# Constant products on TensorE between the gated cell's last transposes and the shared experts' first gate product

## The chip, the core and the metric

The program runs on one core of one Trainium2 chip. The metric is the device time of one execution in microseconds (us). The core has a matrix engine (TensorE, PE in the profile, with its weight loads as PEld), VectorE (DVE), ScalarE (ACT), GpSimd (POOL) and a queue engine that issues transfers (SP). Each runs its own list of instructions in order; they meet through semaphores.

## What is computed

Two gated blocks on 16 sequences of 128 tokens with 256 channels, all in fp32. Cut to what matters here:

```python
x = x + tanh(g_xattn[0]) * L0_xattn(layernorm(x), ctx_1024, ...)   # gated mLSTM cell, 8 heads
x = x + tanh(g_ffn[0])   * L0_ffn(layernorm(x), ...)               # 2 shared + 8 routed experts, top 2
x = x + tanh(g_xattn[1]) * L1_xattn(layernorm(x), ctx_1024, ...)   # attention, 16 heads
x = x + tanh(g_ffn[1])   * L1_ffn(layernorm(x), ...)               # 1 shared + 16 routed experts, top 4

def _ffn(x, w1, w2, w3):                                           # one expert of the first feed-forward
    return jax.nn.silu(x @ w1.T) * (x @ w3.T) @ w2.T
```

The cell divides its weighted values by a normalizer and normalises each token's result. The change lies at the seam between the first line and the second.

## The kernel before

The program is three blocks, one after the other: the front (layer norm and gates, block at L93), the gated cell (block at L310), and everything else (block at L2425). A block holds one list of instructions per engine. At its end the program that the block builder writes has, for every engine, a drain and then a meeting on a semaphore: no engine begins its list of the next block before all have come.

The cell works through eight pairs of sequences. For each pair TensorE makes scores (L393), then the weighted values and row sums (L408, L413), and turns the result back with six transposes against the identity in `cst` (`turn_back`, L428). VectorE then finishes the pair (`finish`, L495 to L516): denominator, reciprocal, two scalings, statistics, and the centred result into `h`. After the last pair TensorE has nothing left in this block, while VectorE still has the last two pairs to finish and ScalarE takes two square roots (L467). Values land in the PSUM banks `pvT[0]` and `pvT[1]`.

In the next block VectorE and ScalarE scale `h` and add it to X (L1877, L1790), VectorE takes statistics of X (L1885, L1888), ScalarE a square root (L1796), and both write the first chunk's normalised tokens (`normalise`, L1899 and L1801). TensorE waits for both (`xn_dve`, `xn_act`), then `turn(0, 0)` and `turn(0, 1)` make four transposes each (L1702) into two banks. ScalarE rounds each bank to fp32r (`keep_hi`, L1807), VectorE takes the rest (`keep_lo`, L1906). `gate_up(0)` waits for the second rest (`lo_ready`) and multiplies 12 times 512 columns of fp32r (L1744 to L1746). The loop then runs `gate_up(u + 1)` ahead of `down(u)` for 32 steps. ScalarE applies silu (L1811) and rounds the hidden values (L1816), VectorE multiplies (L2015) and takes the rest (L2021), TensorE's `down` (L1763) needs both. Operands of `gate_up` and `down` are fp32r; `cst` is a plain fp32 tile of 721 columns.

The routed experts, the attention and the second feed-forward follow in the same block. In the attention the projections of queries and keys (L864) multiply plain fp32 operands over 512 columns, two calls per part. In the front, L171 calls a plain fp32 product of 128 columns 16 times.

Of the kernel before, what the change touches and what calls it, by code (L numbers as in the profile page):

```python
# [51 lines left out]
C_ID, C_PEN, C_BD0, C_PAR, C_REV, C_EPS, C_LNR, C_ONE, C_TRI, C_ONES, C_KEEP, C_STEP, C_TILE = C.values()  # L52
# [225 lines left out]
def cell(nc, X, XNT, ctxT_all, val, v_loaded, m_dram, cst, AT, ET, g_in, g_tanh, lns, ln_tanh, tiles, h, hmv, hstd,  # L278
# [14 lines left out]
    with ExitStack() as ctx:  # L293
# [9 lines left out]
        pvT = two(lambda n: ctx.enter_context(nc.psum_tensor("c_" + n, [128, 512], F32)), "pvT")  # L303
# [8 lines left out]
        def wait(eng, counter, value):  # L312
            if value > 0:
                eng.wait_ge(counter, value)
# [9 lines left out]
        def back_of(i):  # L324

            at = (i - (PAIRS - 2)) * 1024
            return back[:] if at < 0 else score[:, at:at + 1024]

        @block.sync
        def _(sp):  # L330
            for i in range(2, PAIRS):
                wait_expo(sp, i - 2)
                for q in range(2):
                    sp.dma_start(mrow[i % 2][:, q].rearrange("p k r t -> p (k r t)"),
                                 m_dram.rearrange("(b h) t -> b (h t)", b=B)[2 * i + q:2 * i + q + 1]
                                 .broadcast_to([128, NH0 * 128])).then_inc(m_loaded[i % 2], 16)
                if i == 3:
                    sp.dma_start(raw, w0_dram).then_inc(raw_loaded, 16)
            sp.dma_start(xg_dram.rearrange("(p i) d -> p (i d)", p=128),
                         blank_rows.rearrange("(p i) d -> p (i d)", p=128)).then_inc(slots_blank, 16)  # L340
            sp.dma_start(sum_dram[T:T + 128, :], blank_rows[0:128, 0:D]).then_inc(sums_blank, 16)
            sp.wait_ge(split_done, 1)
            sp.dma_start(raw, w1_dram).then_inc(raw1_loaded, 16)
# [39 lines left out]
        @block.tensor  # L383
        def _(pe):
            def scores(i):
                wait(pe, cmat_ready, i)
                for q in range(2):
                    tokens = slice((2 * i + q) * 128, (2 * i + q + 1) * 128)
                    for k in range(KT):
                        for r in range(4):  # L390
                            strip = slice(32 * r, 32 * r + 32)
                            at = r * 512 + (q * KT + k) * 128
                            last = pe.matmul(score[:, at:at + 128], ctxT_all[strip, k, tokens], XNT[strip, k, tokens],  # L393
                                             start=True, stop=True, skip_group_check=True)
                last.then_inc(score_ready, 1)

            def values(i):
                pe.wait_ge(cmat_ready, i + 1)
                for q in range(2):
                    s = 2 * i + q  # L400
                    if i == 0:
                        pe.wait_ge(v_loaded, 16)
                        pe.wait_ge(ones_ready, 1)
                    wait(pe, oT_ready, s - 1)
                    for k in range(KT):
                        for r in range(4):
                            n = 4 * k + r
                            pe.matmul(pvT[q][32 * r:32 * r + 32, k * 128:(k + 1) * 128], val[:, s, n * DH0:(n + 1) * DH0],  # L408
                                      cmat[i % 2][:, q, k, r], start=True, stop=True, skip_group_check=True)
                    for x in range(2):  # L410
                        for r in range(4):
                            n = 2 * r + x
                            last = pe.matmul(pvT[q][32 * r:32 * r + 32, KT * 128:(KT + 1) * 128], one_col[:, x],  # L413
                                             cmat[i % 2][:, q, n // 4, n % 4], start=(x == 0), stop=(x == 1),
                                             skip_group_check=True)
                    last.then_inc(pv_ready, 1)

            def turn_back(i):
                if i < PAIRS - 2:
                    wait(pe, h_ready, i)  # L420
                else:
                    pe.wait_ge(cmat_ready, PAIRS)
                back = back_of(i)
                for q in range(2):
                    pe.wait_ge(oT_ready, 2 * i + q + 1)
                    for k in range(KT + 1):
                        at = q * D + k * 128 if k < KT else 512 + q * 128
                        last = pe.transpose(back[:, at:at + 128], oT[q][:, k],  # L428
                                            cst[:, C_ID:C_ID + 128])
                last.then_inc(back_ready, 1)  # L430

            scores(0)
            for i in range(PAIRS):
                if i + 1 < PAIRS:
                    scores(i + 1)
                if i >= 1:
                    turn_back(i - 1)
                values(i)
            turn_back(PAIRS - 1)

        @block.scalar
        def _(act):
# [1105 lines left out]
def shared_feed_forward(nc, block, sems, X, XN, plain, middle, W, W_hi, x_halves, w_dram, under_tokens, raw1, raw1_loaded, shared, rw, eb, h, hstd, cst, home, slots_blank,  # L1548
# [10 lines left out]
    with ExitStack() as ctx:  # L1559
# [44 lines left out]
        y_bank = [pb(f"y{n}") for n in range(3)]  # L1604
# [19 lines left out]
        def wait(eng, counter, value):  # L1624
            if value > 0:
                eng.wait_ge(counter, value)
# [67 lines left out]
        def _(pe):  # L1694
            def turn(c, half):
                pe.wait_ge(xn_dve, c + 1)
                pe.wait_ge(xn_act, c + 1)
                wait(pe, lo_ready, 2 * c)
                for k in range(KT):
                    for j in range(HALF):  # L1700
                        at = k * 256 + j * 128
                        last = pe.transpose(turned[half][:, at:at + 128], XN[:, c * CH + half * HALF + j, k * 128:(k + 1) * 128],  # L1702
                                            cst[:, C_ID:C_ID + 128])
                last.then_inc(xn_turned, 1)
# [27 lines left out]
            def gate_up(u):  # L1732
                c, n = u // U, u % U
                b, ht, q = n // HT, n % HT, u % 2
                wait(pe, gu_free, u - 1)
                if n == 0:
                    pe.wait_ge(lo_ready, 2 * c + 2)
                if u == HT:
                    pe.wait_ge(block_lo, 3)
                whi, wlo = shared[b]  # L1740
                xhi, xlo = (x_halves[:, c, half] for half in range(2))
                for dst, cols in ((gate, gate_cols), (up, up_cols)):
                    for k in range(KT):
                        pe.matmul(dst[q][:], whi[:, cols(k, ht)], xhi[:, k], start=(k == 0), stop=False)  # L1744
                        pe.matmul(dst[q][:], whi[:, cols(k, ht)], xlo[:, k], start=False, stop=False)
                        last = pe.matmul(dst[q][:], wlo[:, cols(k, ht)], xhi[:, k], start=False, stop=(k == KT - 1))  # L1746
                last.then_inc(gu_ready, 1)

            def down(u):
# [15 lines left out]
                                             start=first, stop=(n == U - 1 and part == 1), skip_group_check=True)  # L1765
                last.then_inc(h_used, 1)

            turn(0, 0)
            turn(0, 1)
            gate_up(0)  # L1770
            for u in range(NU - 1):
                gate_up(u + 1)
# [741 lines left out]
```

## Time and profile before

| | us |
|---|---|
| Median of 3 runs | 856.43 |
| Lowest and highest of the runs | 853.91, 857.67 |
| Span of the profiled execution, first to last instruction | 854.2 |
| TensorE busy | 760.7 (89%) |
| VectorE, ScalarE, GpSimd busy | 503.4, 399.8, 230.6 |

The profiled execution's own time is not listed apart from its span. PEclk is the granted TensorE clock: 1.00 is 2.4 GHz, 0.50 is 1.2 GHz. A product of plain fp32 operands shows as two MATMUL records in the trace, one of fp32r operands or a transpose as one; both kinds carry the type f32. Records of products overlap, so the pace is read from the starts, not from the durations.

### The profile page before, as it was taken

The page shows a single profiled execution, that of the slowest core. Times are in us where ns is not written, and L with a number is a line of the kernel's source. Part 1 is how long each engine was busy: PE and PEld are TensorE (multiplying, and loading weights), DVE is VectorE, ACT ScalarE, POOL GpSimd, SP SyncE. Part 2 cuts the span into 40 slices and gives each one's busy share as a digit, 9 for nine tenths or more (in the row PEclk, how much of TensorE's full clock was granted, in tenths as well). Part 3 has the DMA queues.
Part 4 walks back from the last instruction along what each step waited for, and adds up shares of the span by engine and source line. Part 5 has one row for each costly group of instructions (what it writes and reads, how often), then busy time and mean ns, then how long its engine had stood idle before and what let it go on. Part 6 is the DMA issues. An engine that isn't in the chain of part 4 may idle for free.

```text
span 854.2 us, 15030 instructions
## 1 busy us (share of the span) xinstructions
PE 760.7 (89%) x5266; PEld 615.4 (72%) x5266; DVE 503.4 (59%) x1159; ACT 399.8 (47%) x817; POOL 230.6 (27%) x208
## 2 busy tenths in 40 slices
PE   4567399999998999999999789997779999999997
PEld 3456277788887888888887455655568878888886
DVE  5478865466475333333333787978756665756644
ACT  4399446135363222222233598778635344244232
POOL 0159310027701232233334157663310000000000
PEclk9778789999999999999999999999999999999999
DMA  8379540015252333433332600202004013050140
GB/s 307 92 266 330 220 195 35 1 40 184 88 191 62 64 64 65 89 70 65 67 50 26 229 1 14 87 2 74 2 2 101 1 40 86 0 125 1 25 102 25
DMA packets 37511, 74.46 MB, mean 87 GB/s; under 512 B 4448, under 2 KB 25568, under 8 KB 35680
## 3 DMA queue, kind: packets, MB, share of 16 engines
q1 hardware_dynamic: 30288, 64.16, 24.3%
q0 software_dynamic: 7152, 9.34, 6.0%
q8 instruction: 45, 0.74, 0.4%
q14 instruction: 26, 0.21, 0.1%
HBM read 59.76 MB, written 19.01 MB: 92 GB/s over the span
## 4 chain that ended last, share of the span: by engine, by line
PE 42%; DVE 15%; issue 13%; ACT 7%; POOL 4%; DVEq 4%; DMA 2%; POOLq 0%; ACTq 0%; SPq 0%
PE t_y_ps L2263 8%; POOL slot_tokens L1671 4%; PE a_turned L987 3%; ACT a_hhi L1153 2%; PE a_score L965 2%; PE a_score L967 2%; PE a_score L966 2%; PE t_up L2243 2%; PE t_up L2244 2%; PE t_up L2245 2%; PE t_gate L2233 2%; PE t_gate L2234 2%; PE t_gate L2235 2%; PE a_proj L864 2%; PE t_h_turned L2252 2%
## 5 line engine op out<-in xcount | busy, mean ns | idle before, releaser
L2203 POOL DMA_INDIRECT sums<-t_y,t_dest x39 | 60.9, 1560 | 167.2 <-DMA sums<-t_y,t_dest 111.4
L2298 ACT CAST t_xT_hi<-t_x_turned 128x256 fp32r<-128x256 f32 x39 | 14.5, 372 | 139.0 <-PE t_x_turned L2224 139.0
L2263 PE MATMUL t_y_ps<-W,t_hidT 128*128 x312 | 73.8, 380 | 0.8 <-ACT t_hidT L2308 0.8
L1153 ACT CAST a_hhi<-a_hid 128x512 fp32r<-128x512 f32 x48 | 29.7, 620 | 85.6 <-DVEq L1438 84.0
L2263 PEld LDWEIGHTS t_y_ps<-W,t_hidT 128*128 128x128 f32 x312 | 59.2, 190 | 10.4 <-issue 1.0
L1440 DVE TENSOR_TENSOR a_hlo<-a_hid,a_hhi 128x512 fp32r<-128x512 f32 x48 | 33.2, 692 | 35.1 <-ACT a_hhi L1153 35.1
L1142 ACT ACTIVATE a_act_g<-a_score 128x512 f32<-128x512 f32 x48 | 28.6, 596 | 48.2 <-PE a_score L967 47.6
L820 POOL TENSOR_TENSOR a_sc<-a_sc,a_nmx 128x512 f32<-128x512 f32 x32 | 33.4, 1042 | 55.5 <-DVE a_nmx L1286 55.5
L1102 ACT ACTIVATE a_pr<-a_sc,a_nmx 128x128 f32<-128x128 f32 x128 | 40.9, 391 | 14.3 <-DVE a_nmx L1286 14.2
L2327 DVE TENSOR_TENSOR t_hid<-t_act_g,t_up 128x512 f32<-128x512 f32 x39 | 27.3, 701 | 30.3 <-ACT t_act_g L2303 26.2
L1283 DVE TENSOR_TENSOR a_sc<-a_score,a_pen 128x1024 f32<-128x1024 f32 x32 | 38.9, 1217 | 4.2 <-PE a_score L879 3.1
L1286 DVE TENSOR_REDUCE a_nmx<-a_sc 128x8 f32<-128x1024 f32 x32 | 39.0, 1220 | 2.9
L2338 DVE TENSOR_SCALAR t_y<-t_y_ps,t_dest 128x256 f32<-128x256 f32 x39 | 18.9, 484 | 36.2 <-PE t_y_ps L2263 36.2
L1671 POOL DMA_INDIRECT slot_tokens<-W,slots x32 | 35.5, 1109 | 14.6 <-issue 14.6
L891 PE MATMUL a_turned<-cst,a_pr 128*128 128x128 f32 x256 | 38.9, 286 | 0.5 <-ACT a_prT L1108 0.5
L458 ACT ACTIVATE W<-W,AT 128x128 f32<-128x128 f32 x128 | 38.1, 389 | 2.1 <-POOL W L368 2.1
L903 PE MATMUL a_out_ps<-a_prT,a_v 128*32 128x128 f32 x512 | 25.1, 291 | 15.5 <-issue 11.1
L2233 PE MATMUL t_gate<-whi_main,t_xT_hi 128*128 x78 | 37.1, 476 | 0.3 <-issue 0.2
L2319 DVE TENSOR_TENSOR t_xT_lo<-t_x_turned,t_xT_hi 128x256 fp32r<-128x256 f32 x39 | 16.5, 424 | 31.0 <-ACT t_xT_hi L2298 29.4
L891 PEld LDWEIGHTS a_turned<-cst,a_pr 128*128 128x128 f32 x256 | 27.9, 143 | 9.2 <-issue 6.3
L1432 DVE TENSOR_TENSOR a_hid<-a_score,a_cb 128x512 f32<-128x512 f32 x32 | 22.1, 690 | 20.9 <-PE a_score L967 18.7
L903 PEld LDWEIGHTS a_out_ps<-a_prT,a_v 128*32 128x32 f32 x512 | 11.4, 111 | 31.0 <-issue 24.1
(420 smaller groups left out, 2259.9 us busy)
## 6 DMA issues: line engine op xcount, KB each, us to landing
W<-in_w_dram SPq DMA_DIRECT2D x9, 1536.0 KB, 8.1
a_cb<-comb_rows SPq DMA_DIRECT2D x16, 512.0 KB, 7.6
W<-m_rows SPq DMA_DIRECT2D x14, 512.0 KB, 4.8
slot_tokens<-in_blank_rows_dram SPq DMA_DIRECT2D x1, 5031.0 KB, 20.9
t_x<-slot_tokens SPq DMA_DIRECT2D x39, 129.0 KB, 2.4
a_raw<-in_w_dram SPq DMA_DIRECT2D x3, 1536.0 KB, 6.4
X<-in_x_dram SPq DMA_DIRECT2D x4, 512.0 KB, 5.7
ctxT_all<-in_ctxT_dram SPq DMA_DIRECT2D x4, 512.0 KB, 8.6
```

The lines of the kernel that those rows point to most:

```text
L458: last = act.activation(dmat[i % 2][:, q, k, r], expo[i % 2][:, q, k, r], ACT.Exp, bias=AT[:, at:at + 1], scale=-1.0)
L820: pool.tensor_tensor(part, part, nmx[s % 2][:, g].rearrange("p (i o) -> p i o", o=1).broadcast_to([128, 4, 128]), ALU.add).then_inc(centre ...
L891: last = pe.transpose(turned[n % 2][:, i * 128:(i + 1) * 128], pr[s % 2][:, g, i], cst[:, C_ID:C_ID + 128])
L903: last = pe.matmul(out_ps[32 * i:32 * i + 32, g * 128:(g + 1) * 128], v1[c % 2][:, j, head], prT[g][:, i], start=True, stop=True, skip_gro ...
L1102: last = act.activation(pr[s % 2][:, g, i], sc[s % 2][:, g, i], ACT.Exp, bias=nmx[s % 2][:, g, i:i + 1])
L1153: act.copy(hhi[u % 2][:], hid[u % 2]).then_inc(hhi_ready, 1)
L1283: dve.tensor_tensor(part, score[:, half * 1024:(half + 1) * 1024].rearrange("p (h t) -> p h t", h=8), pen[c % 2][:, j:j + 1].broadcast_to( ...
L1286: dve.tensor_reduce(nmx[s % 2][:, 2 * half:2 * half + 2].rearrange("p r i -> p (r i)"), part, AX.X, ALU.max, negate=True).then_inc(max_rea ...
L1671: pool.indirect_dma_start(xg_dram, bass.IndirectOffsetOnAxis(ap=slots[:, k, s:s + 1], axis=0), XN[:, s, :], None).then_inc(done, 16)
L2203: pool.indirect_dma_start(sum_dram, bass.IndirectOffsetOnAxis(ap=dest[p][:, 0:1].bitcast(U32), axis=0), y[p][:], None, compute_op=ALU.add) ...
L2233: pe.matmul(gate[p][:], xT_hi[p][:, k], W_hi[0][:, ds(e, 1), cols], start=(k == 0), stop=False)
L2263: last = pe.matmul(y_ps[p][:, 0:D], hidT[p][:, h], W[:, ds(e, 1), at:at + D], start=(h == 0), stop=(h == HT - 1))
```

## The change

It adds calls of `pe.matmul` and nothing else. Each multiplies the 128x128 identity of `cst` with the first 512 columns of `cst`, in plain fp32, starts and stops its own sum, and writes a bank whose content nobody reads afterwards: 12 calls at the end of the cell's TensorE list, then in the next block 11 calls ahead of `turn(0, 0)` and 4 between `turn(0, 1)` and `gate_up(0)`. No wait and no semaphore is added on any engine.

```diff
@@ cell, TensorE's list @@
             turn_back(PAIRS - 1)
+            for _ in range(12):
+                pe.matmul(pvT[0][:], cst[:, C_ID:C_ID + 128], cst[:, 0:512], start=True, stop=True)
@@ shared_feed_forward, TensorE's list @@
+            def busy(n):
+                for _ in range(n):
+                    pe.matmul(y_bank[0][:], cst[:, C_ID:C_ID + 128], cst[:, 0:512], start=True, stop=True)
+
+            busy(11)
             turn(0, 0)
             turn(0, 1)
+            busy(4)
             gate_up(0)
```

## Rows read from the trace of the kernel before

**Rows 1.** Windows: length, busy us (instructions) per engine, PEclk, DMA share, GB/s.

```profile
88.00:92.00 4.00, 3.45 (x73) 2.61 (x73) 3.50 (x13) 1.91 (x4) 2.45 (x3) 1.00 0.21 41
94.00:95.00 1.00, 0.00 (x0) 0.00 (x0) 0.78 (x4) 0.00 (x0) 0.00 (x0) 1.00 1.07 442
96.00:98.00 2.00, 0.00 (x0) 0.00 (x0) 1.73 (x6) 0.29 (x1) 0.00 (x0) 0.50 0.06 25
98.00:104.00 6.00, 0.00 (x0) 0.00 (x0) 4.97 (x18) 4.19 (x8) 2.77 (x4) 0.50 0.80 298
112.00:113.00 1.00, 1.00 (x3) 0.75 (x3) 0.00 (x0) 0.00 (x0) 0.00 (x0) 0.50 0.00 0
113.00:116.00 3.00, 3.00 (x15) 2.48 (x14) 1.39 (x3) 1.95 (x5) 0.00 (x0) 0.99 0.00 0
```

**Rows 2.** Timeline, end of the cell: start, us, engine, line, what.

```profile
90.46 1.21 PE L428 MATMUL c_score<-cst,c_oT 128*128 128x128 f32 x6
...
97.06 0.87 DVE L516 SCALAR_TENSOR_TENSOR W<-c_score,hmv,ln_tanh 128x256 f32<-128x256 f32 x2
98.20 0.81 SPq L1639 DMA_DIRECT2D W<-in_w_dram  x2
98.25 0.25 DVE L2037 RECIPROCAL f_hrstd<-hstd 128x16 f32<-128x16 f32 x1 [0.32 <-PEq L293]
```

**Rows 3.** Timeline of PE, the transposes and the first two gate_up at the seam.

```profile
104.41 1.09 PE L1702 MATMUL f_choice<-cst,W 128*128 128x128 f32 x4 [12.74 <-ACT W L1801]
105.29 1.06 PE L1702 MATMUL f_y<-cst,W 128*128 128x128 f32 x4
107.75 0.79 PE L1744 MATMUL f_gate<-x_halves,sw0hi 128*128 128x512 f32 x1 [1.40 <-DVE x_halves L1906]
...
113.04 0.41 PE L1744 MATMUL f_gate<-x_halves,sw0hi 128*128 128x512 f32 x1
...
115.78 0.28 PE L1763 MATMUL f_y<-sw0hi,f_hhi 128*128 128x256 f32 x1
```

**Rows 4.** Timeline of PE, a later pair of turns.

```profile
126.64 0.60 PE L1702 MATMUL f_choice<-cst,W 128*128 128x128 f32 x4
127.07 0.60 PE L1702 MATMUL f_y<-cst,W 128*128 128x128 f32 x4
127.43 0.48 PE L1744 MATMUL f_gate<-x_halves,sw1hi 128*128 128x512 f32 x1
```

**Rows 5.** Timeline of PE, plain fp32 products in the attention: 512 and 256 columns.

```profile
464.48 3.60 PE L864 MATMUL a_score<-a_keyT,a_w 128*128 128x512 f32 x8
467.92 3.62 PE L857 MATMUL a_score<-a_w,a_keyT 128*128 128x256 f32 x16
471.37 3.60 PE L864 MATMUL a_score<-a_keyT,a_w 128*128 128x512 f32 x8
```

**Rows 6.** Front: 16 plain fp32 calls of 128 columns, and the clock over them.

```profile
31.85 6.73 PE L171 MATMUL g_tp<-g_m_row,cst 128*128 128x128 f32 x32 [4.95 <-DVEq L266]
...
36.00:37.00 1.00, 1.00 (x7) 1.00 (x6) 0.36 (x1) 0.00 (x0) 0.00 (x0) 0.50 0.86 119
37.00:38.00 1.00, 1.00 (x7) 1.00 (x7) 0.62 (x1) 0.00 (x0) 0.00 (x0) 0.52 0.70 242
38.00:39.00 1.00, 0.80 (x7) 0.56 (x6) 0.45 (x2) 0.00 (x0) 0.00 (x0) 1.00 0.58 238
```

**Rows 7.** Timeline of ACT and DVE between the turns and the first silu.

```profile
105.53 0.58 ACT L1807 CAST x_halves<-f_choice 128x512 fp32r<-128x512 f32 x1 [1.27 <-PE f_choice L1702]
106.39 0.58 ACT L1807 CAST x_halves<-f_y 128x512 fp32r<-128x512 f32 x1 [0.27 <-PE f_y L1702]
107.00 0.69 DVE L1906 TENSOR_TENSOR x_halves<-f_y,x_halves 128x512 fp32r<-128x512 f32 x1 [0.16 <-ACT x_halves L1807]
109.84 1.28 ACT L1811 ACT_TABLE_LOAD   x1
113.25 0.60 ACT L1811 ACTIVATE W<-f_gate 128x512 f32<-128x512 f32 x1 [2.12 <-PE f_up L1746]
114.65 0.62 ACT L1816 CAST f_hhi<-W 128x512 fp32r<-128x512 f32 x1 [0.80 <-DVEq L2016]
```

**Rows 8.** Waits of PE from 113 to 460: us in total, times, longest.

```profile
PE f_y L1763 <- ACT f_hhi L1816: 2.4, 3, 1.5
PE t_x_turned L2224 <- DMA t_x<-slot_tokens: 1.5, 2, 1.3
PE f_y L2104 <- ACT f_hhi L1816: 0.6, 1, 0.6
PE f_choice L1702 <- DVE W L1899: 0.5, 1, 0.5
PE t_gate L2233 <- issue: 0.2, 1, 0.2
```

## The prediction, made before the changed kernel was run

> **What bounds the kernel now.** I read the windows around the seam first, then the timelines of TensorE, VectorE and ScalarE there, then TensorE's waits behind it. The page says that TensorE is busy 89% of the span, so what matters is whether its idle stretch at the seam is lost, and how fast it runs after it.
>
> The windows show the stretch that the change fills [rows 1]. TensorE's clock is at 1.00 (2.4 GHz) while the cell's last products run, stays there until about 95.9 us with the engine idle since about 91.5, and is then at 0.50 (1.2 GHz) until about 112.8, where it rises after TensorE has been working again since 104.4. The timeline shows who sets the end of the idle stretch. VectorE finishes the cell at 97.93 (97.06 + 0.87), and the first instructions of the next block are at 98.20 and 98.25 [rows 2]: the blocks meet there. Then X, the statistics and the normalised tokens take until 104.3, when TensorE's first transpose can start [rows 3]. VectorE and ScalarE own the path from 91.5 to 107.75; TensorE only fits in its eight transposes. From `gate_up(0)` at 107.75 TensorE is the bound: from 113 to 460 it waits 5.2 us in all (2.4 + 1.5 + 0.6 + 0.5 + 0.2) [rows 8].
>
> What the low clock costs is plain. The 12 products of `gate_up(0)` take 113.04 - 107.75 = 5.29 us, the 12 of `gate_up(1)`, at 2.4 GHz, 115.78 - 113.04 = 2.74 [rows 3]. That is 2.55 us. The eight transposes start their second half 0.88 us after the first, against 0.43 at the high clock [rows 3, 4]; through ScalarE and VectorE this is worth some 0.7 us more. So about 3.2 us can be had at most, 0.4% of the time.
>
> **What one added call costs.** The calls are plain fp32 over 512 columns. The nearest rows are the projections of the attention, the same type and width at the same clock: the group of 8 records at 464.48 is followed by the next at 467.92, so a record takes 3.44 / 8 = 0.43 us, and these 8 records are four calls [rows 5]. One call is 0.86 us. The front says the same of the two records per call: 16 calls of 128 columns are 32 records, 6.73 us at the low clock, 0.42 us a call [rows 6]; four times the columns at twice the clock give 0.84. I take 0.86. At the low clock it would be 1.7.
>
> The Trainium skill ("TensorE: Matmul & The Clock Gate", section "Wait — 56ns, not 53.3ns?") gives 215.7 ns between products of 512 columns at the high clock. By this a call would cost 0.22 us and all 27 together 5.8, with nothing of it on the path; the result would be the first rival's. But the skill's "FP8 and Floating Point Precision" (section "TensorE Precision Notes") says that true fp32 takes four passes, and the rows above agree: 0.86 us for a call.
>
> **The sum, on the profiled execution's clock.**
>
> 1. The cell's 12 calls. The last three transposes are out of the array at about 91.5 (the group of six ends at 91.67, with its tail) [rows 2]. 24 records of 0.43 are 10.3 us: the last starts at 101.4, ends its pace at 101.8, and its tail (a group of eight lasts 3.60, not 3.44 [rows 5]) takes it to 102.0. Until 97.93 they lie beside VectorE's last work and cost nothing. The rest, 4.1 us, has no cover.
> 2. The meeting of the blocks. Every engine drains first, TensorE too, and nobody's list of the next block starts before. That is where these calls are queued ahead of others: SP's three loads, VectorE's reciprocal, ScalarE's and GpSimd's scaling of `h`. With 0.3 us from the last arrival to the first instruction, as now (97.93 to 98.25 [rows 2]), the next block starts at 102.3 and not at 98.2.
> 3. `busy(11)`: 22 records, 9.5 us, 102.3 to 111.8. The normalised tokens, 4.1 us late, are ready at 104.4 + 4.1 = 108.5. The transposes wait 3.3 us for the array.
> 4. Eight transposes at the high clock: 0.86 us (twice 0.43 [rows 4]), to 112.6.
> 5. `busy(4)`: 3.4 us, to 116.1. What it covers is ScalarE's and VectorE's two steps on the second bank: 0.58 + 0.69 with their starts, from about 112.8 to 114.3 [rows 7]. Some 1.7 us stick out.
> 6. `gate_up(0)` starts at 116.1 in place of 107.75: 8.3 later. It runs at 2.4 GHz, as TensorE has had no gap longer than the meeting's: 2.55 back. `gate_up(1)` starts 5.7 us later.
>
> The table load of silu, at 109.84 now, ends 4.8 us after the second turn; it has to be over by 112.8 + 6.2, and is [rows 7]. The first silu waits for the gate product alone, as before. In `down(0)` the rounded values come at 115.27 now, and TensorE is ready for them at 115.78 [rows 3, 7]; both move alike. Behind this I found nothing with a time of its own: the waits in rows 8 are for engines and transfers that hang on the same chain, GpSimd's scattering and SP's weight loads included, so the shift is kept. Bounds: fully kept, +5.7; at the other end TensorE's waits for ScalarE and VectorE in rows 8 vanish, 2.4 + 0.6 + 0.5 = 3.5 us, and the meeting costs nothing of its own, 0.4 (second rival): +1.8. I take 5.7, since each of those waits names a producer that is itself late.
>
> The span of 854.2 becomes 859.9. What lies around the span isn't shown and doesn't change; the runs lie from 0.3 below the span to 3.5 above, their median 2.2 above. On the median: 856.4 + 5.7 = **862.1 us**, 0.67% slower.
>
> **The rivals.**
>
> *The calls are cheap and the clock pays.* If a call costs one pace of a record, 0.43 us, the 12 end at 96.7, ahead of VectorE; the 11 run from 98.3 to 103.0; the clock stays high. The first transposes retire at 104.41 + 0.60, the second at 105.44, the two ScalarE steps end at 106.2, VectorE's at 107.05, and the 4 calls end at 107.0. `gate_up(0)` starts 0.7 earlier and runs 2.55 shorter: -3.2, **853.2 us**, within 0.5%, not slower. It decides at one price: solving 91.5 + 0.3 + 0.2 + 27 p + 0.86 = 107.75 + 2.55 gives p = 0.65 us a call. Rows 5 and 6 stand at 0.86 and 0.84. Chance 0.06.
>
> *The meeting doesn't wait for TensorE's array.* If TensorE's list passes the drain when its products are issued, nobody else is held at 98.2, but the 23 calls still stand in line before the first transpose: 91.5 + 19.7 = 111.2, gate_up(0) at 115.5, +7.8 - 2.55 = +5.2, **861.6 us**. The trace can't exclude it: in both meetings that it shows another engine came last. The result is nearly the same, as TensorE's own work is then the path. Chance 0.08.
>
> *The tail soaks it up.* TensorE's later waits [rows 8] shrink because the other engines got a head start while it ran constants: around +3, **859.5 us**, within 0.5%. Against it: most of these waits are behind work that itself starts from a product. Chance 0.13.
>
> *Constants don't keep the clock.* If the grant falls to 1.2 GHz at 95.9 as now, the remaining 14 records of the first 24 and the 30 after cost 0.86 each: gate_up(0) would start near 135 and run slow, +27, 884 us. In the front the clock rose to 1.00 at about 38.0 after 6 us of just such products against `cst` [rows 6]. Chance 0.03.
>
> **How the numbers follow.** The forecast has 0.68, the rivals 0.06, 0.08, 0.13 and 0.03, and 0.02 is left for what I don't see. The range: downward to the bound of the kept shift, 858.2; upward 1.7 for a short stretch at the low clock (two calls at 0.86 more each), 0.5 for a later release at the meeting and 1.2 for the spread of the runs above their median: 862.1 + 1.7 + 0.5 + 1.2 = 865.5. That leaves out the cheap calls and the slow clock, 0.09, and a little of the rest. A measurement of this kernel can tell about 0.5% from no change, 4.3 us, so slower means above 860.7. The forecast is there nine times in ten with the runs' spread (0.61), the second rival likewise (0.07), the third now and then (0.02), the slow clock always (0.03): slower 0.73. Faster by 4.3 us needs more than the clock can give: 0.02. Same: 0.25.
>
> **What the profile would show.** Step 1: 24 records of the new line after 91.5, 0.43 apart, the last near 101.4. Step 2: SP's first load and VectorE's reciprocal near 102.2; at 98.2 the second rival holds. Step 3: 22 records from 102.3 to 111.8 and transposes that wait for nothing but their own engine. Step 5: the first gate product right behind the last constant one, near 116.1. Step 6: PEclk at 1.00 from 84 to well past 120 and 2.7 us for `gate_up(0)`. TensorE's waits in rows 8 unchanged speak against the soaking up. One record per call, or records 0.22 apart, would make the prediction wrong at its root, and the time about 853.

## The result, and the profile after

The changed kernel takes 862.73 us (median of 6 runs, 860.36 to 865.47); the kernel before, run beside it, 854.22 (853.14 to 857.67). The ratio is 1.0081, with a 95% interval of 1.006 to 1.0103: between 5.1 and 8.8 us slower. The ratio alone says 6.9 us, the two medians lie 8.5 apart; both are in the interval. The forecast was 862.1 us and 5.7 slower. The profiled execution has a span of 858.5 us.

The stretches that were shown of before, now of after (length, busy us of PE, PEld, DVE, ACT and POOL, PEclk, DMA share, GB/s):

```profile
88.00:92.00 4.00, 3.88 (x73) 2.74 (x66) 3.50 (x13) 2.24 (x3) 1.55 (x2) 1.00 0.36 87
94.00:95.00 1.00, 1.00 (x3) 0.38 (x2) 0.91 (x3) 0.00 (x0) 0.00 (x0) 1.00 0.84 356
96.00:98.00 2.00, 2.00 (x6) 0.83 (x5) 1.02 (x4) 0.30 (x1) 0.00 (x0) 1.00 0.00 0
98.00:104.00 6.00, 5.70 (x14) 2.39 (x13) 2.30 (x7) 2.20 (x5) 0.42 (x1) 1.00 0.27 70
112.00:113.00 1.00, 1.00 (x4) 0.45 (x3) 0.74 (x2) 1.00 (x3) 0.00 (x0) 1.00 0.95 393
```

TensorE is busy where it was idle, and PEclk is 1.00 in all five, while the last three of them stood at 0.50 in before [rows 1]. The clock came as wished. What it cost is in VectorE's column of the fourth row: 2.30 us of work between 98 and 104, against 4.97 before. VectorE was kept out.

The timelines of after (start, us, engine, line, what, idle time before it) show how. This execution reaches the end of the cell 0.79 us earlier than the one of before did (96.27 against 97.06 for VectorE's last pair [rows 2]), so the times of the two are compared from there.

```profile
90.72 10.46 PE L441 MATMUL c_pvT<-cst 128*128 128x512 f32 x24
96.27 0.88 DVE L518 SCALAR_TENSOR_TENSOR W<-c_score,hmv,ln_tanh 128x256 f32<-128x256 f32 x2
101.43 0.81 SPq L1641 DMA_DIRECT2D W<-in_w_dram  x2
101.48 0.25 DVE L2045 RECIPROCAL f_hrstd<-hstd 128x16 f32<-128x16 f32 x1 [4.34 <-PEq L293]
...
101.48 9.68 PE L1772 MATMUL f_y<-cst 128*128 128x512 f32 x22 [0.30 <-PEq L293]
111.00 0.60 PE L1704 MATMUL f_choice<-cst,W 128*128 128x128 f32 x4
111.44 0.60 PE L1704 MATMUL f_y<-cst,W 128*128 128x128 f32 x4
111.87 3.60 PE L1772 MATMUL f_y<-cst 128*128 128x512 f32 x8
114.91 0.79 PE L1746 MATMUL f_gate<-x_halves,sw0hi 128*128 128x512 f32 x1
...
118.04 0.39 PE L1746 MATMUL f_gate<-x_halves,sw0hi 128*128 128x512 f32 x1
```

The 12 calls are 24 records and last until 101.18, 4.0 us past VectorE's end at 97.15. Every engine starts the next block at 101.4 to 101.5, and VectorE's 0.32 us of waiting for the meeting [rows 2] is 4.34. Then 22 records, the transposes right behind them, 8 records, and `gate_up(0)` right behind those. From VectorE's last pair in the cell to the first product of `gate_up(1)` it was 113.04 - 97.06 = 15.98 us before [rows 2, 3] and is 118.04 - 96.27 = 21.77: **+5.79 us**. This distance is used below for each experiment, as the shift at the seam. It is free of what happens before and behind.

### The profile page after: what moved, and what is told of

It reads as the page before. It is cut to its first block, busy times and chain, and to the rows that moved or that the text cites. A ratio compares the mean times of both kernels' runs of the same rounds, so it can differ in the third digit from the quotient of the medians.

```text
span 858.5 us, 15138 instructions
## 1 busy us (share of the span) xinstructions
PE 777.8 (91%) x5320; PEld 620.4 (72%) x5320; DVE 505.5 (59%) x1159; ACT 399.8 (47%) x817; POOL 228.7 (27%) x208
## 4 chain that ended last, share of the span: by engine, by line
PE 43%; DVE 14%; issue 13%; ACT 7%; POOL 4%; DVEq 4%; DMA 2%; POOLq 0%; ACTq 0%; SPq 0%
PE t_y_ps L2271 8%; POOL slot_tokens L1673 4%; PE a_turned L989 2%; PE a_turned L893 2%; ACT a_hhi L1155 2%; PE a_score L967 2%; PE a_score L969 2%; PE a_score L968 2%; PE t_up L2253 2%; PE t_up L2251 2%; PE t_up L2252 2%; PE t_gate L2241 2%; PE t_gate L2242 2%; PE t_gate L2243 2%; PE a_proj L866 2%
```

## The experiments

All keep the changed kernel's positions of the calls; the last one adds a place. Ratios are against runs of the kernel before on the same chip: 25 runs with a median of 855.46 us for the first four experiments, 35 with 855.76 for the others. In the profiles the time of a run is its span and 1.8 to 1.9 us around it.

**One half at a time.** First only the 12 calls of the cell:

```diff
-            busy(11)
             turn(0, 0)
             turn(0, 1)
-            busy(4)
             gate_up(0)
```

> Only the 12 calls at the end of the cell. My theory: 24 records of 0.43 us hold the meeting of the blocks for 4.1 us (as the trace of after shows: SP and VectorE start 4.3 us after VectorE's last instruction in place of 0.3), then TensorE idles about 6.5 us until the first transposes, so its clock falls again and gate_up(0) takes 5.3 us: +4.1 us, ratio 1.0048. Rival (the meeting does not cost anything, only the line before the transposes does): +0, ratio 1.000. Rival (the clock survives the 6.5 us): +0.9, ratio 1.001.

Measured: ratio 1.0049 (1.0032 to 1.0066), 859.21 us. The meeting is where it was said to be:

```profile
96.04 0.88 DVE L518 SCALAR_TENSOR_TENSOR W<-c_score,hmv,ln_tanh 128x256 f32<-128x256 f32 x2
101.25 0.25 DVE L2043 RECIPROCAL f_hrstd<-hstd 128x16 f32<-128x16 f32 x1 [4.33 <-PEq L293]
107.40 1.09 PE L1704 MATMUL f_choice<-cst,W 128*128 128x128 f32 x4 [6.45 <-ACT W L1807]
110.74 0.79 PE L1746 MATMUL f_gate<-x_halves,sw0hi 128*128 128x512 f32 x1 [1.40 <-DVE x_halves L1912]
...
115.09 0.39 PE L1746 MATMUL f_gate<-x_halves,sw0hi 128*128 128x512 f32 x1
```

VectorE waits 4.33 us for the meeting, TensorE idles 6.45 us, and the clock falls: it is at 0.50 when the transposes run. The 24 records end at 100.95, and VectorE starts 0.30 us later, as it started 0.32 after its own last work before. So the end of the block does wait for TensorE's products, and these 12 calls alone make the kernel slower. At the seam the shift is 19.05 - 15.98 = +3.1, not +4.1, because the clock rose within `gate_up(0)`, which took 4.35 us and not 5.3.

Then only the 11 and the 4 calls of the next block:

```diff
             turn_back(PAIRS - 1)
-            for _ in range(12):
-                pe.matmul(pvT[0][:], cst[:, C_ID:C_ID + 128], cst[:, 0:512], start=True, stop=True)
```

> Only the 11 and the 4 calls of the next block. My theory: the meeting is at 98.2 as before; the 11 calls begin at the low clock at 1.7 us each and go on at 0.86 once the clock has risen after some 5 us: the transposes start near 110.3 in place of 104.4, gate_up(0) near 114.6 at the high clock: +6.9 - 2.55 = +4.3 us, ratio 1.005. Rival (only what holds the meeting costs): -3.2 us, ratio 0.996, the clock gain alone.

Measured: ratio 1.0076 (1.0052 to 1.0099), 861.30 us, from four runs.

```profile
97.78 11.24 PE L1770 MATMUL f_y<-cst 128*128 128x512 f32 x22 [6.58 <-PEq L293]
108.86 0.60 PE L1702 MATMUL f_choice<-cst,W 128*128 128x128 f32 x4
```

The 22 records take from 97.78 to 108.86, the meeting is undisturbed, and the shift at the seam is (115.92 - 96.58) - 15.98 = +3.4. The clock rose after about 3 us of the calls, earlier than the 5 I had put, hence less than the 4.3 expected. Over the whole run the loss is larger than at the seam, 6.5 us with an interval of 4.4 to 8.5. The trace, of the fastest of the four runs, does not show this: from VectorE's last pair to its end it is 857.5 - 96.58, against 854.2 - 97.06 before, 3.8 us more. Where the rest is lost stays open. The rival of a pure gain is out.

**So many calls as have cover.** By the sum, 7 calls fit ahead of VectorE's end, 7 ahead of the tokens, 2 beside the last two steps.

```diff
-            for _ in range(12):
+            for _ in range(7):
...
-            busy(11)
+            busy(7)
             turn(0, 0)
             turn(0, 1)
-            busy(4)
+            busy(2)
```

> The same calls, but 7, 7 and 2 of them, so many as have cover at 0.86 us a call: 7 end at 97.5, ahead of VectorE's last instruction; 7 run from 98.3 to 104.3, ahead of the tokens; 2 lie beside the two steps of ScalarE and VectorE. My theory: nothing is held, the clock stays at 2.4 GHz: -3.2 us, ratio 0.9963. Rival (constant products cost something of their own beside the array's time, or the clock's gain is lost behind the seam): 0 or slower, ratio 1.000 or above.

Measured: ratio 0.9978 (0.996 to 0.9995), 853.81 us. It is faster than both kernels, though than the one before only by 0.4 to 3.4 us. In its trace:

```profile
90.98 6.17 PE L441 MATMUL c_pvT<-cst 128*128 128x512 f32 x14
96.53 0.88 DVE L518 SCALAR_TENSOR_TENSOR W<-c_score,hmv,ln_tanh 128x256 f32<-128x256 f32 x2
97.73 0.25 DVE L2045 RECIPROCAL f_hrstd<-hstd 128x16 f32<-128x16 f32 x1 [0.32 <-PEq L293]
97.73 6.25 PE L1772 MATMUL f_y<-cst 128*128 128x512 f32 x14 [0.57 <-PEq L293]
103.90 0.63 PE L1704 MATMUL f_choice<-cst,W 128*128 128x128 f32 x4
106.52 0.50 PE L1746 MATMUL f_gate<-x_halves,sw0hi 128*128 128x512 f32 x1
...
109.38 0.39 PE L1746 MATMUL f_gate<-x_halves,sw0hi 128*128 128x512 f32 x1
```

The meeting costs VectorE 0.32 us as before, `gate_up(0)` takes 2.9 us, and the shift at the seam is 12.85 - 15.98 = **-3.13**, where -3.2 was expected. The time itself was expected at a ratio of 0.9963 and gained less (below). The constants are harmless where they have cover; only the count was wrong.

**The same calls at another price.** The 12, 11 and 4 calls over 256, 384 and 128 columns:

```diff
-pe.matmul(pvT[0][:], cst[:, C_ID:C_ID + 128], cst[:, 0:512], start=True, stop=True)
+pe.matmul(pvT[0][:, 0:256], cst[:, C_ID:C_ID + 128], cst[:, 0:256], start=True, stop=True)
...
-pe.matmul(y_bank[0][:], cst[:, C_ID:C_ID + 128], cst[:, 0:512], start=True, stop=True)
+pe.matmul(y_bank[0][:, 0:256], cst[:, C_ID:C_ID + 128], cst[:, 0:256], start=True, stop=True)
```

> The change with its 12, 11 and 4 calls, each over 256 columns in place of 512, at 0.43 us a call: the first rival of the prediction made true. My theory, that the price of a call decides and turns at 0.65: -3.2 us, ratio 0.9963. If the number of calls or records is what costs, it stays slower than before, towards +5.7 us, ratio 1.007.

Measured: ratio 0.9977 (0.9963 to 0.9991), 853.22 us; shift at the seam -3.13. The same number of calls is free at half the columns. The price goes by the columns: the cell's 24 records last 5.35 us here, 7.91 over 384 columns (next) and 10.46 over 512.

> The 12, 11 and 4 calls over 384 columns, 0.645 us a call, at the price where my sum turns its sign (0.65). My theory: the meeting is some 1.5 us late, the 11 calls stick out 1 us past the tokens, the 4 calls 0.9 past ScalarE's and VectorE's steps, and the clock gives 3.2 back: 0 us, ratio 1.000 against 0.9977 at 256 columns and 1.0081 at 512. If the calls cost in proportion to their columns from the first on, it would lie midway between the two, 1.003.

Measured: ratio 1.0025 (0.9998 to 1.0052), 857.42 us. The interval holds both 1.000 and the rival's 1.003: the time alone doesn't decide between them. The trace does:

```profile
96.99 0.88 DVE L518 SCALAR_TENSOR_TENSOR W<-c_score,hmv,ln_tanh 128x256 f32<-128x256 f32 x2
99.63 0.25 DVE L2045 RECIPROCAL f_hrstd<-hstd 128x16 f32<-128x16 f32 x1 [1.77 <-PEq L293]
99.64 7.33 PE L1772 MATMUL f_y<-cst 128*128 128x384 f32 x22 [0.30 <-PEq L293]
106.81 0.60 PE L1704 MATMUL f_choice<-cst,W 128*128 128x128 f32 x4
...
113.03 0.39 PE L1746 MATMUL f_gate<-x_halves,sw0hi 128*128 128x512 f32 x1
```

The meeting is 1.45 us late (1.77 against 0.32), and the shift at the seam is 16.04 - 15.98 = +0.06 us, against -3.13 at 256 columns and +5.79 at 512. Midway between these two would be +1.3. So at 0.645 us a call the clock's gain is just used up at the seam, and up to 256 columns nothing is paid.

> The 12, 11 and 4 calls over 128 columns, 0.215 us a call: TensorE then idles some 3.9 us ahead of the meeting and some 3.8 ahead of the first transposes. In the kernel before the clock fell 4.4 us after the last product. If such gaps are short enough here, the clock stays and the time is that of 256 columns, ratio 0.9977. If it falls in either gap, gate_up(0) takes 5.3 us again and the ratio is 1.000. I hold the second a little likelier, as the constants are then a quarter of the engine's time.

Measured: ratio 0.9977 (0.9957 to 0.9996), 855.00 us; shift at the seam -3.13. What I held a little likelier didn't come, though the clock did fall. Windows of this trace (columns as above):

```profile
94.00:97.00 3.00, 0.00 (x0) 0.00 (x0) 2.65 (x8) 0.29 (x1) 0.00 (x0) 1.00 0.33 139
98.00:99.00 1.00, 1.00 (x9) 1.00 (x8) 1.00 (x4) 1.00 (x4) 0.00 (x0) 0.71 0.69 135
99.00:101.00 2.00, 2.00 (x11) 1.93 (x10) 1.82 (x7) 1.64 (x2) 1.64 (x3) 0.50 0.94 387
102.00:104.00 2.00, 0.57 (x5) 0.60 (x6) 2.00 (x6) 1.09 (x2) 0.14 (x1) 1.00 1.04 442
```

TensorE idled 3.90 us to 97.25 and the clock fell at about 98.4, already within the 11 calls; these ran at 1.2 GHz to 101.2, and the clock was back ahead of the first transposes at 103.43. The slow calls had cover.

**Without the last calls.** 7 and 7, none ahead of `gate_up(0)`:

```diff
             turn(0, 1)
-            busy(2)
             gate_up(0)
```

> 7 and 7 calls, none between the transposes and gate_up(0). My theory: that gap is 1.5 us and the clock was high, so it stays and gate_up(0) takes 2.7 us: the same as with 7, 7 and 2, ratio 0.9978. If the last calls are what keeps the clock, gate_up(0) takes 5.3 us: ratio 1.000 or 0.999.

Measured: ratio 0.9978 (0.9958 to 0.9998), 854.53 us; shift at the seam (109.33 - 96.50) - 15.98 = -3.15. A gap of 1.56 us there does no harm in this trace, and the last calls can go.

**Where the rest of the gain goes.** Four versions gain 3.1 us at the seam, and their ratios say some 1.9, with intervals that hold 3.1. One loss stands in the traces of all of them. The 7, 7 and 2 version first, then before:

```profile
108.61 1.28 ACT L1819 ACT_TABLE_LOAD   x1
109.91 0.60 ACT L1819 ACTIVATE W<-f_gate 128x512 f32<-128x512 f32 x1
117.48 0.39 PE L1765 MATMUL f_y<-sw0hi,f_hhi 128*128 128x256 f32 x1 [1.04 <-ACT f_hhi L1824]
...
120.81 0.39 PE L1763 MATMUL f_y<-sw0hi,f_hhi 128*128 128x256 f32 x1 [0.69 <-ACT f_hhi L1816]
```

Before, ScalarE had loaded silu's table 2.12 us ahead of the first silu, which waited for TensorE [rows 7]. Now `gate_up(0)` is done so early that the first silu starts right behind the load, 0.3 us later than TensorE allows: it starts 0.2 us after the first product of `gate_up(1)` in before and after (113.25 and 113.04, 118.24 and 118.04), and 0.53 here (109.91 and 109.38). TensorE waits 0.35 us longer for it in `down(1)`. The later pair of turns, at 126.64 in before [rows 4], is at 123.31 here, so that (123.31 - 96.53) - (126.64 - 97.06) = -2.80 of the -3.13 are left; the 256 column, 128 column and 7 and 7 versions have the same wait of 1.04. The gain that can reach the end of the kernel is thus 2.8 us, not 3.1. This is read from the traces; no run moves the load.

A second loss, further on, is in the traces of the 7, 7 and 2 version, of the 128 column version and of both halves alone. It comes at the start of the attention (7, 7 and 2 version, timeline of PE, then windows):

```profile
476.50 1.06 PE L854 MATMUL a_turned<-cst,a_pr 128*128 128x128 f32 x8 [2.64 <-ACT a_pr L1092]
477.40 3.26 PE L859 MATMUL a_score<-a_w,a_keyT 128*128 128x256 f32 x8
...
474.00:476.00 2.00, 0.00 (x0) 0.00 (x0) 1.49 (x9) 1.03 (x3) 0.00 (x0) 1.00 1.08 364
478.00:480.00 2.00, 2.00 (x6) 1.59 (x5) 1.07 (x5) 0.46 (x2) 0.49 (x2) 0.50 1.02 426
```

Eight records take 3.26 us at the low clock. In after there was a gap of the same length at this place and no fall:

```profile
484.13 1.06 PE L854 MATMUL a_turned<-cst,a_pr 128*128 128x128 f32 x8 [2.65 <-ACT a_pr L1092]
485.03 1.89 PE L859 MATMUL a_score<-a_w,a_keyT 128*128 128x256 f32 x8
```

So two calls of 512 columns, 1.7 us, were put into that gap, on top of the 256 column version:

```diff
+                if part == (0, "x", 0):
+                    for _ in range(2):
+                        pe.matmul(bank, cst[:, C_ID:C_ID + 128], cst[:, 0:512], start=True, stop=True)
                 if kind == "x":
                     pe.wait_ge(rows_dve, c + 1)
```

> The 256 column version and two constant products of 512 columns more, 1.7 us, at the start of the attention, where TensorE waits 2.3 to 2.6 us for the first tokens. In the traces of three of the experiments the clock fell for 3.4 us right there and the next products took 1.4 us longer; before, after and the 256 column version didn't show it. If that fall is where the gain of these runs went, this version has no fall there in its trace, and is 0 to 1.8 us faster than the 256 column version: ratio 0.9960 to 0.9977. Rival: the falls further on (at the end of the attention) set the rest, and this one gives nothing: 0.9977.

Measured: ratio 0.9976 (0.9953 to 1.000), 854.23 us, no fall at that place in its trace, and the same shift at the seam, -3.13. It is not to be told from the 256 column version. That version had no fall there in its own trace either, nor had the 7 and 7 version, which gains no more than the others, so the traces do not show that the two calls did anything. A loss of 1.4 us in some executions is below what these intervals can show, so whether this fall takes what is missing beside the 0.3 us of the table load stays open, and so does whether more is missing at all. From VectorE's last pair to the end of the span the five traces with -3.13 or -3.15 at the seam are 0.2 to 3.5 us shorter than before's: one trace a version is not enough to follow one microsecond over 750.

## Why the prediction was right

*The price of a call.* 0.86 us was taken from the attention's products [rows 5], and 24 records last 10.46 us, 0.43 each. This is the step on which all hung: with the price halved (256 columns) the same 27 calls bring -3.13 us at the seam. The first rival was a true account of another price: it said -3.2 us there, and its turning point of 0.65 us was met by 384 columns with +0.06. That its 853.2 us and the 853.22 of the 256 column run agree is chance: the rival counted 3.2 us from 856.4, the run's ratio of 0.9977 is 2.0 us from 855.46.

*The meeting.* The sum said, on before's times, that the last product ends at 102.0 and that the next block starts at 102.3. This execution is 0.79 us earlier, so that is 101.2 and 101.5 here, and the trace has 101.18 and 101.48. The second rival, a meeting that doesn't wait for the array, is out: VectorE waits 4.34 us in after and 4.33 with the 12 calls alone. It had the same result, since TensorE's own line was then the path, so its chance did not bear on the number.

*The line before the transposes.* 111.8 was said, which is 111.0 here, and they start at 111.00. The transposes' waiting shows on ScalarE, 4.13 us idle until `f_choice`. After the transposes come 8 records, and `gate_up(0)` was said for 116.1 - 0.79 = 115.3. Its first record is at 114.91, overlapping the tail of the last constant, and the second at 115.54, one pace of 0.23 behind 115.3.

*The clock.* 2.55 us back in `gate_up(0)`: 118.04 - 115.3 = 2.7 us for its 12 products, as at the high clock before [rows 3]. The rival that constants don't hold the clock is out.

*The tail.* The shift was to be kept, and TensorE's waits in the same stretch of after are unchanged against [rows 8]:

```profile
PE f_y L1765 <- ACT f_hhi L1824: 2.4, 3, 1.5
PE t_x_turned L2232 <- DMA t_x<-slot_tokens: 1.6, 2, 1.2
PE f_y L2112 <- ACT f_hhi L1824: 0.7, 1, 0.7
PE f_choice L1704 <- DVE W L1907: 0.5, 1, 0.5
```

In this stretch nothing was soaked up, and at the start of the attention the shift is still (485.03 - 96.27) - (479.92 - 97.06) = 5.90. Behind it 0.8 us of it goes, and why stays open: the spans differ by 858.5 - 854.2 = 4.3, and 5.1 with the 0.79. The runs say 6.9 with an interval from 5.1. The seam's 5.79 lies in between. The sum's 5.7 was right at the seam to 0.1 us. That its median, 862.1, was met to 0.6 is in part luck: the six runs of before have a median 2.2 below the three that it was counted from, and the medians lie 8.5 apart and not 5.7, so that a start too high and a shift too small made up for each other.

*What was off.* When the clock rises. For the two halves run alone I expected the rise too late, and both shifts at the seam came out 1 us too high, 4.1 for 3.1 and 4.3 for 3.4. In the forecast itself the clock never fell, so this didn't enter. Two readings of the prediction were wrong, also without effect on the sum. In before the clock rises at 113.05 and not at 112.8: the whole window from 112 to 113 is at 0.50 [rows 1]. And the first silu doesn't wait for the gate product alone but for the up product behind it, as its row says [rows 7]. The limit of 3.2 us took no account of silu's table load, which takes 0.3 of it back.

## What to carry to other kernels

Filler work for an idle matrix engine has to be counted in its true time: a plain fp32 product of 512 columns held this engine for 0.86 us, nearly four times as long as an fp32r one (0.23), and 27 of them are 23 us, for some 14 us of idle time (91.5 to 97.9, 98.3 to 104.4, and the last two steps ahead of `gate_up(0)`). Count the room up to each meeting and each operand's arrival separately, and stay below it; a call too many at the end of a block delays every engine, since the block's end waits for the products. Before adding filler, work out the most that it can bring, and look at what the faster engine will then wait for: here 3.1 us of 855 at the seam, of which a table load on another engine left 2.8. 14 calls of 512 columns brought as much as 27 of 256.

## What the runs showed of the hardware that was not expected

The clock doesn't fall at a fixed time after the last product. It fell 4.5 us after it in before (91.5 to 96.0); about 3 us after it with the 12 calls alone (last product at 100.95, PEclk 0.86 between 103 and 104) and with the next block's calls alone (last product at 91.2, PEclk 0.55 between 94 and 95); about 5 us after it, and 1.2 us after work had begun again, with 128 columns. At the start of the attention a gap of 2.65 us left the clock high in after, while a gap of 2.64 in the 7, 7 and 2 version and one of only 2.24 with the 12 calls alone were followed by a fall. Its rise varies as well: it came after 3 us of constants with the next block's calls alone, within `gate_up(0)` 6.6 us after the transposes began with the 12 calls alone, and 8.6 us after they began in before [rows 1, 3]. The executions of one kernel differ too: those of the 256 column version have a mean clock of 0.982 and 851.76 us at one end and of 0.972 and 856.99 us at the other. The clock is not all of it: one with 0.982 took 854.71.
